# Leaving out the zero array tiles of the steps inside tiles, and a new order of the array tiles in every step

## The reference

```python
e = jnp.stack([tbl_0[ids[:, 0]], ..., tbl_39[ids[:, 39]]], axis=1)   # 2048 x 40 x 64
viW = jnp.einsum('bpd,pde->bpe', e[:, i_idx, :], W)                  # W: 780 x 64 x 64
z = jnp.einsum('bpe,bpe->bp', viW, e[:, j_idx, :])                   # 2048 x 780
h = jnp.concatenate([z, dense_ctx], axis=1)
h = jnp.maximum(h @ W_top1 + b_top1, 0.0)                            # 796 -> 512
h = jnp.maximum(h @ W_top2 + b_top2, 0.0)                            # 512 -> 256
y = h @ W_top3                                                       # 256 -> 1
```

## Time and profile before

| what | value |
|---|---|
| median of 3 runs | 1225.1 us (1223.88 to 1225.45) |
| the profiled execution | 1221.73 us, its span 1219.9 us |
| TensorE (PE) busy | 1156.4 us, 95% |
| VectorE (DVE) busy | 972.9 us, 80% |
| ScalarE (ACT) busy | 879.3 us, 72% |
| GpSimd (POOL) busy | 606.9 us, 50% |
| mean granted TensorE clock | 0.992 |

### The profile page before, as it was taken

One profiled execution on the slowest core, in us unless ns is written; L12 is line 12 of the kernel. 1 busy time (PEld: TensorE's weight loads), 2 busy tenths in 40 slices (PEclk: granted clock), 3 DMA queues, 4 the chain that ended last, 5 costly groups with the idle time before them and its releaser, 6 DMA issues.

```text
span 1219.9 us, 51509 instructions
## 1 busy us (share of the span) xinstructions
PE 1156.4 (95%) x20872; PEld 500.6 (41%) x20872; DVE 972.9 (80%) x850; ACT 879.3 (72%) x6754; POOL 606.9 (50%) x647
## 2 busy tenths in 40 slices
PE   1699999999999999999999999999999999999988
PEld 0256656776433333333343333333334343333333
DVE  0389898999677788999867778999967888899950
ACT  0287977788567688788856677888856777888861
POOL 6776677277773667777755666777720000000000
PEclk9799999999999999999999999999999999999999
DMA  4244444444322323332332223232221221112001
GB/s 136 61 117 132 135 134 131 122 127 125 101 76 78 86 75 82 81 84 61 105 75 75 77 77 97 69 83 82 73 70 60 65 64 54 57 56 72 20 2 47
DMA packets 54342, 101.40 MB, mean 83 GB/s; under 512 B 14420, under 2 KB 14420, under 8 KB 54104
## 3 DMA queue, kind: packets, MB, share of 16 engines
q1 hardware_dynamic: 29520, 67.19, 17.1%
q0 software_dynamic: 20560, 21.34, 9.2%
q10 hardware_dynamic: 4024, 9.58, 2.6%
HBM read 98.05 MB, written 0.01 MB: 80 GB/s over the span
## 4 chain that ended last, share of the span: by engine, by line
PE 69%; issue 9%; DVE 8%; POOL 8%; ACT 3%; DMA 3%; DVEq 0%; ACTq 0%; POOLq 0%
PE u L763 28%; PE zacc L778 14%; PE u L759 13%; PE u L813 8%; POOL gathered L521 6%; DVE prod L689 4%; ACT row_prod L589 3%; DMA gathered<-tbl,index 3%; DVE row_prod L657 3%; PE u L732 2%; PE u L816 2%; POOL first_fields L521 1%; DVE row_prod_v L657 1%; DVE row_sums L698 1%; PE u L819 1%
## 5 line engine op out<-in xcount | busy, mean ns | idle before, releaser
L589 ACT ACTIVATE row_prod<-row_prod 128x64 f32<-128x64 f32 x3328 | 796.3, 242 | 115.6 <-DVE row_prod L657 111.2
L689 DVE TENSOR_TENSOR prod<-u,emb 128x1024 f32<-128x1024 f32 x544 | 642.0, 1218 | 188.3 <-PE u L763 187.1
L589 ACT ACTIVATION_READ_ACCUMULATOR row_prod<-row_prod 128x1 f32 x3328 | 624.8, 188 | 0.0
L521 POOL DMA_INDIRECT gathered<-tbl,index x512 | 484.3, 946 | 215.1 <-issue 141.5
L763 PE MATMUL u<-emb,weights 64*32 64x512 f32 (+1 forms) x10880 | 572.0, 510 | 4.1 <-ACT emb L548 1.2
L763 PEld LDWEIGHTS u<-emb,weights 64*32 64x32 f32 x10880 | 221.4, 107 | 275.4 <-issue 149.2
L778 PE MATMUL zacc<-prod,band 64*32 64x512 f32 (+1 forms) x5240 | 309.0, 505 | 2.2 <-issue 0.9
L759 PE MATMUL u<-weights,emb 64*32 64x512 f32 x4096 | 287.9, 594 | 3.2 <-DVE prod L689 1.2
L657 DVE TENSOR_TENSOR row_prod<-u,first_fields 128x1024 f32<-128x1024 f32 x208 | 253.1, 1217 | 9.1 <-PE u L759 8.2
L778 PEld LDWEIGHTS zacc<-prod,band 64*32 64x32 f32 x5240 | 119.9, 107 | 139.7 <-issue 121.0
L521 POOL DMA_INDIRECT first_fields<-tbl,index x128 | 121.1, 946 | 71.3 <-issue 35.5
(11 more groups left out here) (21 smaller groups left out, 62.7 us busy)
## 6 DMA issues: line engine op xcount, KB each, us to landing
weights<-w_pairs SPq DMA_DIRECT2D x205, 320.0 KB
gathered<-tbl,index POOLq DMA_INDIRECT x512
w12s<-w_top ACTq DMA_DIRECT2D x16, 448.0 KB, 3.4
first_fields<-tbl,index POOLq DMA_INDIRECT x128
w12s<-w_top ACTq DMA_DIRECT2D x8, 256.0 KB, 2.7
index<-ids POOLq DMA_DIRECT2D x1, 320.0 KB, 5.1
z<-dense ACTq DMA_DIRECT2D x4, 32.0 KB
y<-h ACTq DMA_DIRECT2D x4, 2.0 KB
```

What stands on the lines that cost most here:

```text
L521: pool.indirect_dma_start(out=to, out_offset=None, in_=tables[2 * t + e], in_offset=bass.IndirectOffsetOnAxis(ap=index[:, col:col + 1].bit ...
L589: last = nc.scalar.activation(x, x, ACT.Copy, accum_out=row_sums[:, s, q:q + 1])
L689: nc.vector.tensor_tensor(result, products, x, ALU.mult).then_inc(prod_ready, 1)
```

## The change

Set A is exactly the set of tiles whose weights are zero in a half step. The change leaves their matmuls out there, 4 of 8, and in every step (col, half and row) issues the tiles of set A first. As quarters of `u` are now read by VectorE's product without having been written in that step, the whole of `u` is set to zero once at the start; TensorE's first instruction waits for one memset more.

```diff
+TILE_ORDER = [(0, 0), (0, 1), (1, 2), (1, 3), (0, 2), (0, 3), (1, 0), (1, 1)]
...
         def _(dve):
+            dve.memset(u[:, :, :, :], 0.0).then_inc(band_made, 1)
             dve.memset(band[:, :], 0.0).then_inc(band_made, 1)
-            dve.wait_ge(band_made, 1)
+            dve.wait_ge(band_made, 2)
             dve.memset(band[:, TILE - 1:TILE], 1.0).then_inc(band_made, 1)
...
-                    for h, g in itertools.product((0, 1), range(TILES)):
+                    for h, g in TILE_ORDER:
+                        if part[0] == "half" and (h == 0) == (g < TILES // 2):
+                            continue
                         half = slice(h * DIM, (h + 1) * DIM)
                         of = slice(g * TILE, (g + 1) * TILE)
...
             pe.wait_ge(ident_made, 2)
-            pe.wait_ge(band_made, 2)
+            pe.wait_ge(band_made, 3)
```

## The result

The changed kernel took 1223.11 us (median of 21 runs), the kernel before 1225.43 us in 21 runs beside it: a ratio of 0.9984 with a 95% interval of [0.9977, 0.9991], so 2.0 us faster (1.1 to 2.8; one run of each kernel, 1248 and 2959 us, was far slower than all its others and is not in the interval). Forecast were 1222.8 us and a gain of 2.3. The two profiled executions can't show this as a difference of spans: the one of before was a short one of its kind (1221.73 us where its runs lie around 1225), the one of after took 1223.22. Stretches of the two can be compared, and that is what the rest does.

A forecast was written before the change was run, and what follows sets the result against it. PE was taken to set the pace in much of the kernel, with DVE or gathers elsewhere. Terms 0.75 + 0 + 1.3 + 0.3 + 0 = 2.35 us took 1225.1 to 1222.8 us, range 1219.8 to 1225.7.

The forecast's parts named there:

- The fullest tile sets the length: Between array-mode changes, slots (0.86 us) of the fullest tile count; five stretches lose slots, at most 6.9 us.
- Chunk 1 to 2, 1.3 us: Sum 65 to transpose (2, 6): 1.72 us of slots, less 0.15 for a buffer and 0.25 for a gather.
- Chunk 2 to 3, 0.3 us: Before step (3, 3): transpose 1.6 us earlier, but 1.3 goes into waiting for ScalarE's copy; gain 0.3 us.
- Middle of chunk 0, 0.75 us: From sum 33 to the transpose: 0.75 us of one 0.86 us slot gained and kept.
- Chunk 0 to 1, 0: End of chunk 0: a 0.86 us slot, but a transpose waits for a gather landing at 359.0; gain 0.
- Chunk 3's end, 0: Last steps before the final turn: DVE-bound, so PE waits longer by what it gains; gain 0.
- The order, 0, and the memset, 0: Naming set A first moves no work; the start's memset, at most 5.4 us, is hidden; 0 each.
- the clock: No term in the sum; the tail before the last turn at another clock was listed as a sign of being wrong.
- the first (all slots, 4 us or more): Rival: all slots come through at the five stretches, gain 4 to 6.9 us (1218.2 to 1221.1); chance 0.13.
- the second (no change): Rival: tiles don't run far enough ahead or gains fall into gathers; gain under 0.7 us; chance 0.18.
- the third: Rival: slower, as steps wait their turn behind each of 272 sums in the new order; 1227.4 us; chance 0.11.

The follow-up runs named there:

- e2: Changed kernel, but set A's matmuls left out only in the other eight half steps of a chunk, kept in the last two; 1.0006 of the kernel before, +0.7 us.
- e3: Changed kernel with everything left out but tiles issued in the old order; 0.9992 of the kernel before, -1.0 us.
- e1: Changed kernel, but set A's matmuls left out only in the last two half steps of a chunk; 1.0004 of the kernel before, +0.5 us.
- e6: Kernel before, nothing left out, old order, with most half-column sums outside the last group moved to set A; 1.0001 of the kernel before.
- e4: Changed kernel's new tile order alone, nothing left out; 1.0000 of the kernel before.
- e8: Changed kernel with LANDING 11 for 9, transposes two steps later; 0.9901 of the kernel before, -12.1 us.
- e7: Kernel before with LANDING 11 for 9, transposes two steps later; 0.9933 of the kernel before, -8.2 us.
- e5: Changed kernel with most half-column sums outside the last group moved to set A; 0.9979 of the kernel before, -2.6 us.
- e12: Changed kernel with LANDING 13 for 9, on the third chip; 0.9916 of the kernel before, which took 1751.9 us there.

## Why the prediction came out as it did

The time (1223.1 against 1222.8) and the sign were right. Its steps one by one:

- *The fullest tile sets the length.* Right where it was tested by place: 7.86 became 6.29 us from sum 65 to transpose (2, 6) (6.1 to 6.3 forecast), and from chunk 2 to 3 the 6.15 us of the earlier trace rows became 898.46 - 893.93 = 4.53, for which 6.15 - 1.6 was written. e2 shows the other half: half steps elsewhere give nothing at the chunks' ends. The Trainium skill (TensorE: Matmul & The Clock Gate, Part 3, "What overlaps and what doesn't") has matmuls start in program order. This trace disagrees with it: a MATMUL of step (1, 198) starts at 601.46, and the next ones of sum 65, which stands ahead of the step, at 601.83.
- *Chunk 1 to 2, 1.3 us.* The slots were right, the term for the gather was mis-sized: I charged 0.25 us within 0 to 1.5. The gather took 5.63 us to land, where I had taken 3.3 as likely from gathers of 2.50 to 4.72, and PE stood 1.32 us. Of 1.57 us only 0.1 to 0.2 were left at product 406 (1.60 against 1.77 at 397). This is one execution. In e3 the same wait is 0.67 us and 0.67 are kept, and in e1 it is 0.31 and 1.11 are kept, so after's 0.17 is at the low end and 1.3 above all three.
- *Chunk 2 to 3, 0.3 us.* Right in kind, and 0.53 instead of 0.3 (e1 0.46, e3 0.47). Step (3, 3) waits for ScalarE's copy behind row reductions, as said, but 0.36 us and not 1; the transpose itself waited 0.37 us for a gather first, which I didn't have (PE's timeline of after, then ACT's):

```profile
898.46 0.66 PE L735 MATMUL u<-ident,gathered 128*128 128x128 f32 x4
899.48 0.66 PE L735 MATMUL u<-ident,gathered 128*128 128x128 f32 x4 [0.37 <-DMA gathered<-tbl,index]
900.07 1.95 PE L769 MATMUL u<-emb,weights 64*32 64x512 f32 x32
902.38 1.09 PE L769 MATMUL u<-emb,weights 64*32 64x512 f32 x16 [0.36 <-ACT emb L550]
```

```profile
901.32 1.00 ACT L550 ACTIVATE emb<-u 128x1024 f32<-128x1024 f32 x1
```

- *Middle of chunk 0, 0.75 us.* 1.04 in after, 1.07 in e2, 1.06 in e3, where one slot is 0.86. Kernels that leave nothing out at step (0, 103) scatter more than at the chunks' ends (e1 gains 0.20, e6 loses 0.40, e4 1.14), so more than the slot may be in it by chance. At product 150 after still has it.
- *Chunk 0 to 1, 0.* Not settled. From product 197 to 207 after gains 0.78 us, and e1, which has the same slot, 0.20; in both, PE stands for gathers there (0.33 and 0.67 us). But e6, with nothing left out, gains 0.69 there too, so no part of after's 0.78 can be put down to the slot.
- *Chunk 3's end, 0.* Right. The last products are 0.85 us earlier, and PE's idle time before the turn is longer by more, beside the earlier trace rows:

```profile
1172.60 0.61 PE L769 MATMUL u<-emb,weights 64*32 64x512 f32 x4
1178.83 1.94 PE L795 MATMUL u<-ident,row_sums 128*128 128x128 f32 x8 [5.61 <-issue]
```

- *The order, 0, and the memset, 0.* e4 has 1.0000. The memset took 2.62 us (at most 5.4 written), and DVE's first product starts at 31.38, before at 31.41.
- *What was missing: the clock.* The sum had no term for it; I had named it for the tail alone. After's profile is at half clock for 3.4 us at 70 us and for 3.4 at 588, where before is not, and for 6.8 instead of 3.4 us at the end. The first two cost 1.4 us (1.50 less the 0.10 by which the wait there grew, 2.34 beside 2.24) and 1.2; at the end it is 0.35 (span 1.49 longer, product 799 0.29 later, and the 0.85 that the turn doesn't follow). How much of that the change brings in the mean isn't shown. E6, with nothing left out, has the fall at 588 too, and the timed runs can't be priced by their mean clock: over the 20 of after it is 0.9906, which is 23 us at half clock beside the 18 and 20 of before on the first two chips, but the 17.1 us near the start weigh most in it. Four of after's runs at 0.996 take 1222.9 us in the mean and seven at 0.989 take 1222.7, where 0.35 us for each us would put 6 us between them.

So the forecast of 2.3 was near the measured 2.0 partly by luck. The stretches of after's table keep 1.04 + 0.17 + 0.53 = 1.7 us of the 2.35, with the middle of chunk 0 higher than written, chunk 1 to 2 much lower and chunk 2 to 3 a little higher, and a loss by the clock that no term had stands against them, somewhere between the tail's 0.35 us and the 3.0 us of after's profile. These can't be added up to the measured 2.0, since they come from single executions and the interval is 1.7 us wide.

Of the rivals, the first (all slots, 4 us or more) is excluded by the interval of after, though e8 beside e7 doesn't exclude it for late transposes; the second (no change) is excluded by the interval of after, the third by e4.

## What to carry to other kernels

Where an engine is split into tiles, count the work of the fullest tile between two points at which all tiles must be done; that says where leaving work out can help and gives the upper end of it. Then look at what PE meets there: here each slot gained ran into a gather or a copy with little slack, and moving the transposes two steps back, one number, was worth four times as much (8.2 us) as the change (2.0). When a faster stretch ends in front of a wait, price that wait by its longest landing, and give the slower clock that can follow it a term of its own. And profile the kernel before more than once: its one profile here was a short run whose clock didn't fall in the middle, so falls that e6 has without the change looked like losses of the change.

## What the runs showed of the hardware

- PE's clock fell to 1.2 GHz in the middle of the kernel at single waits for gathers (in e1, e2 and e3 before the wait had ended), and 3.4 or 6.8 us later it was back. At transpose (2, 5) it stayed at full clock with waits of 1.66 (before), 1.85 (e8) and 2.33 us (e4), and fell with 2.37 (e5), 2.47 (e3), 2.50 (after), 2.78 (e2) and 3.11 (e1), but with 2.02 (e6) too. In chunk 0 near 69 us it fell with 2.34 (after), 2.44 (e5) and 2.46 (e2) and not with 2.48 (e6), 2.70 (e7), 2.94 (e8) and 2.95 us (e3). So the length of the wait doesn't decide by itself; what else does was not tried.
- A sum on set A and the half step behind it on set B ran beside each other with 0.06 to 0.07 us between their starts (after, e1, e3, e5). Where the half step used all eight tiles it was 0.91 to 0.92 us (before, e2, e4).
- One of the three chips ran the kernel before at 1752 us instead of 1224, its clock at 0.948 in the mean, and in e12's profile MATMULs start in pairs 0.7 us apart there. Results from that chip can't be set beside those of the others.
